# Two reorderings in a four-batch transformer block: the first feed-forward portions of an attention pass, and VectorE's copies of smoothing states at the joint between batches

## What is computed

```
xn  = layernorm(x)
x1  = layernorm(xn[:, :, :128] + attention_1(xn[:, :, :128]))       # 8 heads of 16
xs  = holt(xn)        # smoothing along the tokens: level and trend carried from token to token
x2  = layernorm(xs[:, :, :128] + attention_2(xs[:, :, :128]))
y   = concatenate(x1, x2)
out = x + layernorm(y + relu(y @ w_ff1.T + b_ff1) @ w_ff2.T + b_ff2)
        + relu(xn @ W1 + b1) @ W2 + b2                               # the "second net"
```

## Time and profile before

| what | value |
|---|---|
| median of 3 runs | 2519.6 us (2518.51 to 2520.58) |
| the profiled execution's own time | 2518.65 us |
| its span, first to last instruction | 2517.1 us |
| TensorE busy | 2449.2 us, 97% |
| ScalarE busy | 2181.0 us, 87% |
| VectorE busy | 1342.0 us, 53% |
| GpSimd busy | 382.6 us, 15% |
| mean granted TensorE clock | 0.993 |

### The profile page before, as it was taken

The page is one execution under the profiler, slowest core; times in us unless marked ns, Lnnn a source line. Parts: engine busy times, 40 slices in busy tenths (PEclk is TensorE's granted clock), DMA queues, the critical chain, the costliest instruction groups (busy, mean ns, idle before and its releaser), DMA issues.

```text
span 2517.1 us, 66734 instructions
## 1 busy us (share of the span) xinstructions
PE 2449.2 (97%) x29057; PEld 963.6 (38%) x29057; DVE 1342.0 (53%) x3059; ACT 2181.0 (87%) x2419; POOL 382.6 (15%) x375
## 2 busy tenths in 40 slices
PE   6899999999999999999999999999999999999995
PEld 4233333336633333334653333333564333333354
DVE  5344445557734445555774444444676444455576
ACT  5899999986499999997569999999657999999952
POOL 1200110003510020000440002000063000100053
PEclk9999999999999999999999999999999999999998
DMA  8100220006110030000610003000151001200001
GB/s 222 56 19 18 46 41 12 6 6 129 51 44 18 19 61 10 10 6 6 145 60 19 18 18 62 10 10 6 58 93 52 10 10 30 42 10 10 6 30 44
DMA packets 49677, 95.96 MB, mean 38 GB/s; under 512 B 7888, under 2 KB 32464, under 8 KB 48992
## 3 DMA queue, kind: packets, MB, share of 16 engines
q1 hardware_dynamic: 42880, 76.92, 11.2%
q0 software_dynamic: 6496, 14.69, 3.7%
HBM read 57.45 MB, written 34.08 MB: 36 GB/s over the span
## 4 chain that ended last, share of the span: by engine, by line
PE 92%; ACT 3%; DVE 2%; DMA 1%; POOL 1%; issue 1%; SPq 0%; DVEq 0%; ACTq 0%; POOLq 0%
PE slot L1492 37%; PE slot L1466 22%; PE slot L1252 17%; PE slot L1525 5%; PE slot L1541 5%; PE slot L1370 2%; ACT p_sb L744 1%; POOL p_sb L618 1%; PE slot L1379 1%; PE slot L1317 1%; PE slot L1361 1%; PE slot L1355 1%; PE slot L1334 1%; ACT area L759 1%; ACT p_sb L760 1%
## 5 line engine op out<-in xcount | busy, mean ns | idle before, releaser
L744 ACT ACTIVATE p_sb<-slot 128x1024 f32<-128x1024 f32 x2048 | 1902.2, 1029 | 61.6 <-PE slot L1466 61.6
L1492 PE MATMUL slot<-p_sb,v_sb 128*17 128x512 f32 x8192 | 1068.0, 595 | 6.4 <-ACT p_sb L744 6.0
L1466 PE MATMUL slot<-q_st,k_st 50*128 50x512 f16 x4096 | 621.5, 382 | 6.1 <-ACT p_sb L744 3.2
L1466 PEld LDWEIGHTS slot<-q_st,k_st 50*128 50x128 f16 x4096 | 117.1, 94 | 875.0 <-ACT p_sb L744 870.7
L923 DVE SCALAR_TENSOR_TENSOR second<-slot,second 128x256 f32<-128x256 f32 x64 | 27.2, 425 | 594.0 <-PE slot L1252 594.0
L1492 PEld LDWEIGHTS slot<-p_sb,v_sb 128*17 128x17 f32 x8192 | 181.7, 96 | 222.9 <-ACT p_sb L744 205.3
L911 DVE TENSOR_SCALAR hid_one<-slot,b_grown 128x256 f32<-128x256 f32 x256 | 123.9, 484 | 235.4 <-PE slot L1252 234.6
L1252 PE MATMUL slot<-w_parts,hid_parts 128*32 128x256 f16 x6144 | 214.9, 274 | 0.0
L1252 PE MATMUL slot<-xt_parts,w_parts 128*32 128x256 f16 x6144 | 214.8, 274 | 0.0
L1252 PEld LDWEIGHTS slot<-w_parts,hid_parts 128*32 128x32 f16 x6144 | 141.4, 96 | 110.0 <-issue 108.6
L1252 PEld LDWEIGHTS slot<-xt_parts,w_parts 128*32 128x32 f16 x6144 | 141.1, 96 | 110.3 <-issue 108.6
(11 more groups left out here) (117 smaller groups left out, 1734.9 us busy)
## 6 DMA issues: line engine op xcount, KB each, us to landing
part_dram<-p_sb SPq DMA_DIRECT2D x16, 1024.0 KB, 4.1
xn<-x SPq DMA_DIRECT2D x16, 512.0 KB, 4.9
second<-x SPq DMA_DIRECT2D x32, 256.0 KB, 3.1
ffn_dram<-second SPq DMA_DIRECT2D x32, 256.0 KB, 2.0
area<-ffn_dram SPq DMA_DIRECT2D x16, 512.0 KB, 5.3
out<-area SPq DMA_DIRECT2D x15, 512.0 KB, 3.3
k_st<-part_dram SPq DMA_DIRECT2D x24, 256.0 KB, 11.6
k_st<-part_dram POOLq DMA_DIRECT2D x48, 128.0 KB, 3.9
```

Source lines behind the costliest of these rows:

```text
L744: act.activation(p_sb[:, n % 4, :], slot[n % 3][:, :], ACT.Exp, scale=0.25 / GROW ** 2).then_inc(exp_done, 1)
L1466: mm = pe.matmul(slot[at % 3][:, k * CHUNK:(k + 1) * CHUNK], k_st[rows_, pair, kt * P:(kt + 1) * P], q_st[rows_, pair, c_ * CHUNK:(c_ + 1) ...
L1492: mm = pe.matmul(o_bank[ROW * j:ROW * j + DK + 1, :], v_sb[:, a, kt, GH * g + j, :], p_sb[:, n % 4, (j % 2) * CHUNK:(j % 2 + 1) * CHUNK], ...
```

## The change

Two things are moved. No instruction is added or taken away but one semaphore wait on TensorE.

1. In unit 0 of each batch's attention the first portion of the second net's hidden layer goes from key step 4 to key step 0, and the others go from 6, 7, 9, 10, 12, 13, 14 to 5, 7, 8, 10, 11, 13, 14. Since portion 0 now stands ahead of the wait of p·v for the fourth quarter's `ff_read`, it gets that wait itself.
2. In the joint VectorE copies the local states ahead of the first half of the inverse, state 2 ahead of the second half, and state 3 (with `state_read`) ahead of `attended`.

```
-FIRST_HIDDEN_KTS = [4, 6, 7, 9, 10, 12, 13, 14]
+FIRST_HIDDEN_KTS = [0, 5, 7, 8, 10, 11, 13, 14]
...
                         second_sums()
+                        local_states()
                         invert(0)
-                        local_states()
+                        next_state(2)
                         invert(1)
-                        next_state(2)
-                        attended(before, UNITS2 - 1)
                         next_state(3)
                         state_read()
+                        attended(before, UNITS2 - 1)
                         check_sums(before, UNITS2 - 1)
                         add_projection(before, UNITS2 - 1)
...
                 def second_hidden(b, i, k):
                     h = HALVES * b + i
+                    if i == 0 and k == 0:
+                        pe.wait_ge(ff_read, CHUNKS * b + 2)
```

## The result

The changed kernel takes 2527.08 us in the median of 9 executions (2522.91 to 2528.35), the kernel before 2520.41 (9 executions, 2518.51 to 2522.03). The ratio is 1.0025, with a 95% interval of 1.0015 to 1.0036: slower, by 6.7 us, where 4.4 were forecast, and outside the stated range.

What follows compares the result with a forecast made beforehand. TensorE was taken to bound the kernel, with 92% of the chain. Three joints +3.45, unit 0 in batches 1 to 3 +0.45 and batch 0 +0.5 gave +4.4 us: forecast 2524.0 us, range 2520.8 to 2526.5.

Steps and rivals of the forecast that it cites:

- What bounds the kernel, and that the early copies gain nothing: TensorE holds 92% of the chain and does not idle in the joint; copies are early enough, so making them earlier gains nothing.
- What the new order does to VectorE: In the joint, VectorE idles 1.1 us ahead of state 3's copy; `attended` ends at 567.57 instead of 564.77.
- What TensorE then waits for: In each joint, 0.6 us ahead of the out-projection and 0.5 ahead of the transposes: 1.15 us, +3.45 for three.
- Given back later?: Behind the joint TensorE idles hardly at all until the next attention, so no later wait absorbs the joint's loss.
- Unit 0: Attention's first unit, portions at new key steps: +0.15 us a batch, +0.45 for batches 1 to 3; +0.5 in batch 0.
- Sum: Whole kernel: 3.45 + 0.45 + 0.5 = +4.4 us, 2523.05 on the profiled execution, 2524.0 as median.
- the third rival: In the joint, waits could take TensorE's clock to 1.2 GHz: 1.3 us a joint, 3.9 more, 2527.9 us; chance 0.04.
- The range: Whole kernel's time from 2520.8 to 2526.5 us, leaving out about 2 in 10.

Runs made afterwards that it cites:

- The two early moves alone: Kernel before with local states copied ahead of the inverse's first half, state 2 ahead of its second, state 3 still behind `attended`: 2520.47 us, ratio 1.0000.
- the first group of experiments: Changed kernel unaltered, its portions alone, its VectorE order alone, and that order without state 3's move, on one chip; 33 executions of the kernel before there: median 2520.5 us.
- The filled kernel: Changed kernel plus three idle matmuls on TensorE in the joint, two ahead of the out-projection, one ahead of the transposes: 2522.81 us, ratio 1.0011.
- the copies alone: Kernel before with only VectorE's new copy order in the joint, portions as before: 2526.14 us, ratio 1.0025.
- the long execution: Profiled execution of the changed kernel run again unaltered: 2528.05 us at mean clock 0.991; that run's median is 2527.23 us.
- the second wait alone: Kernel before with `check_sums` done twice in the joint, so TensorE waits only ahead of the transposes: 2522.35 us, ratio 1.0009.
- the split `attended`: Changed kernel with the first of the two multiplications in `attended` moved ahead of state 3's copy: 2522.36 us, ratio 1.0009.

## Why the prediction was wrong

- *What bounds the kernel, and that the early copies gain nothing*: right. The two early moves alone measure 1.0000.
- *What the new order does to VectorE*: right to 0.1 us. An idle 1.16 us ahead of the last copy (1.1 forecast), released by TensorE's own state matmul.
- *What TensorE then waits for*: right in sum, 1.15 us a joint as forecast. The waits are 0.64 and 0.38 us by the profile's own count of idle, which takes the modelled end of the matmul ahead; the forecast had 0.6 and 0.5.
- *Given back later?* No, as forecast.
- *Unit 0*: +0.16 us in batch 1 (0.15 forecast) with gaps at 14, 20, 26, 32, and +0.46 in the opening (0.5 forecast).
- *Sum*: 2523.05 for an execution like the profiled one of before. The changed kernel's profiled one, with no fall in its joints, took 2522.91, and its three others at a mean clock of 0.993 took 2523.6 to 2524.2. In the first group of experiments the 19 executions of before at 0.993 have a median of 2519.6 us and the three of the changed kernel one of 2523.8: 4.1 us apart, where the sum is 4.4. The filled kernel's nine at 0.993 stand 3.1 us above the like ones of before, under the sum by 1.3 us, for which no row was found.
- **The step that failed is that the two waits cost their own length and nothing more: the sum has no term for the clock.** The clock's fall was the third rival, given 0.04 on one row: around the start of batch 1's attention TensorE idles for 0.61 us and its clock stays at 1.00. That row was no evidence for the joint. What was shown in its place: of 20 executions of the changed kernel, 16 have the lower mean clock and take 2526 us or more; in the two traces that have a fall in a joint, one long one and one of the copies alone, it sits at the waits; filling the waits brings 4.2 us back with nothing else moved. Its price was too low as well: 1.3 us for a fall, measured 1.6 and 2.7, because the slow stretch takes in the transposes. The rival had a fall in all three joints, the long execution has it in two; too many falls at too low a price nearly cancel, and that its 2527.9 comes near the measured 2527.1 is luck.
- *The range* left the clock out for this reason, and so ended at 2526.5.

## What to carry to other kernels

A short wait on TensorE is not always priced by its own length: 0.64 and 0.38 us in each of three joints cost 3.45 us by the rows and, in most executions, some 4 more through the clock, and whether one profile shows it is a matter of luck, so set the mean clocks of all executions beside their times. A copy that can't come before another engine's signal should not stand ahead of work that is ready; VectorE's program is in order, and everything behind it is late by the whole wait. Where such a wait can't be avoided, useless matmuls in it can be the cheaper way: one small matmul in each joint was enough here.

## What the hardware did that I had not expected

The fall depends on the place and not only on the length: 0.64 us behind `smoothing` and ahead of the out-projection let the clock fall, alone (2525.4) or with the 0.38 behind it (2527.2), while 0.81 us ahead of the transposes (2522.4) did not, nor did 0.61 us at the attention's start in any trace. In one and the same execution two joints fell and one did not, with the same waits. What about the work ahead of the wait makes the difference was not tried and stays open. The kernel before has executions at a mean clock of 0.991 too (6 of the 33 in the first group, 2521.1 to 2521.7), so it is not free of falls elsewhere. One such place shows in three of the traces, those of the second wait alone, of the three fillers and of the split `attended`: the start of the last batch's nets, where TensorE waits 2.4 us in every kernel. Here it is with the second wait alone (timeline, then TensorE's windows):

```profile
2404.88 6.36 PE L1526 MATMUL slot<-area,wf_parts 128*128 128x512 f16 x21 [2.38 <-DVE area L947]
```

```profile
2405.00:2407.00 2.00, 2.00 (x6) 0.50 0.19 74
```

The profiled executions of the kernel before and of the changed kernel have the same wait and a clock of 1.00 behind it. So the same wait lets the clock fall in one execution and not in another, there as in the joint. Whether these falls are the ones in the executions of before with the lower mean clock is not shown.
